# Second layer of a graph kernel: the one-hots of a row move from SBUF to a PSUM bank, but for the last sixteen rows

## The reference

```python
x = _layernorm(x + _L0_gnn_ref(x, src, dst, edge_weight, L0_gnn_W), axis=-1)
x = _layernorm(x + _L1_gnn_ref(x, edge_index, edge_attr_9, L1_gnn_w0, ..., L1_gnn_w4), axis=-1)
```

## Time and profile before

| | |
|---|---|
| median of 3 runs | 4325.02 us (4324.73 to 4326.77) |
| the profiled execution | 4325.59 us, of which the span from first to last instruction 4323.8 us |
| mean granted TensorE clock | 0.752 of full speed |
| busy over the span | PE 56%, DVE 49%, ACT 33%, POOL 68% |
| second layer, first gather to last | from 1529 us to 4299 us |

### The profile page before, as it was taken

One profiled execution on the slowest core, in us unless ns is written; L12 is line 12 of the kernel. 1 busy time (PEld: TensorE's weight loads), 2 busy tenths in 40 slices (PEclk: granted clock), 3 DMA queues, 4 the chain that ended last, 5 costly groups with the idle time before them and its releaser, 6 DMA issues.

```text
span 4323.8 us, 55250 instructions
## 1 busy us (share of the span) xinstructions
PE 2407.8 (56%) x15332; PEld 2127.3 (49%) x15334; DVE 2119.4 (49%) x4356; ACT 1419.8 (33%) x2142; POOL 2955.5 (68%) x2887
## 2 busy tenths in 40 slices
PE   2200399999999934545444444454544454445555
PEld 1000399999999823434343434343434343434444
DVE  8999788888888732222222222222222222223333
ACT  5444466666666521111111111111111111112222
POOL 5100277777777567777777777777777777777775
PEclk6555699999999867767777767776777776767767
DMA  1000233333333322212122112111211221212222
GB/s 56 7 0 19 83 95 95 95 101 96 95 95 100 110 64 54 55 49 53 49 54 54 49 54 54 49 54 48 54 54 48 54 54 48 54 49 66 78 74 59
DMA packets 116447, 268.24 MB, mean 62 GB/s; under 512 B 50449, under 2 KB 50593, under 8 KB 115233
## 3 DMA queue, kind: packets, MB, share of 16 engines
q0 software_dynamic: 92080, 191.02, 16.6%
q1 hardware_dynamic: 19698, 68.09, 4.5%
q10 hardware_dynamic: 4608, 8.39, 0.5%
HBM read 252.30 MB, written 8.72 MB: 60 GB/s over the span
## 4 chain that ended last, share of the span: by engine, by line
POOL 48%; issue 15%; PE 1%; POOLq 0%; DMA 0%; DVE 0%; ACT 0%; DVEq 0%
POOL feat L1562 48%; PE quad L1727 1%; POOLq L1558 0%; DMA feat<-x,ids 0%; PE mixed L1739 0%; POOLq L1559 0%; ACT z_last L1666 0%; DVE group L1871 0%; DVE dst_col L1956 0%; POOLq L1552 0%; DVE z_last L1967 0%; DVE stats L1970 0%; POOLq L1556 0%; POOLq L1510 0%; DVE mv L1973 0%
## 5 line engine op out<-in xcount | busy, mean ns | idle before, releaser
L1562 POOL DMA_INDIRECT feat<-x,ids x2048 | 2146.5, 1048 | 636.4 <-issue 635.8
L1727 PE MATMUL quad<-attr_hot,feat 128*128 128x144 f32 x4096 | 926.3, 409 | 1407.0 <-DMA feat<-x,ids 854.2
L1727 PEld LDWEIGHTS quad<-attr_hot,feat 128*128 128x128 f32 x4096 | 862.7, 295 | 1479.4 <-issue 1476.9
L1871 DVE TENSOR_TENSOR group<-group,quad 128x504 f32 (+1 forms) x512 | 348.0, 680 | 1907.3 <-PE quad L1727 1869.3
L1137 POOL DMA_INDIRECT l_feat<-in_x,id_of x768 | 727.3, 947 | 601.2 <-ACT w_of L830 366.7
L1579 ACT ACTIVATE quad<-quad 128x1008 uint32<-128x1008 uint32 x258 | 256.6, 995 | 2030.3 <-DVE group L1871 2030.3
L1739 PE MATMUL mixed<-group,mix 128*128 128x384 f32 x1152 | 411.2, 514 | 17.9 <-DVE group L1871 17.9
L1039 DVE TENSOR_SCALAR keys<-swap,src_of,w_of 128x184 f32<-128x184 f32 x1024 | 326.9, 389 | 92.6 <-PE l_pre L1230 92.6
L1039 DVE TENSOR_SCALAR w_row<-swap,src_of,w_of 128x184 f32<-128x184 f32 x1024 | 327.3, 390 | 51.6 <-PE l_pre L1230 49.6
L1847 DVE TENSOR_TENSOR attr_hot<-hot,attr_e 128x2304 f32<-128x2304 f32 x128 | 327.5, 2559 | 4.4
L1739 PEld LDWEIGHTS mixed<-group,mix 128*128 128x128 f32 x1152 | 234.1, 208 | 169.4 <-issue 46.1
(11 more groups left out here) (249 smaller groups left out, 2390.7 us busy)
## 6 DMA issues: line engine op xcount, KB each, us to landing
place<-table SPq DMA_DIRECT2D x64, 640.0 KB
feat<-x,ids POOLq DMA_INDIRECT x2048, 2.5
l_feat<-in_x,id_of POOLq DMA_INDIRECT x768
attr_in<-in_edge_attr SPq DMA_DIRECT2D x18, 576.0 KB, 3.9
norm_x<-in_x SPq DMA_DIRECT2D x16, 256.0 KB, 2.7
x<-norm_z ACTq DMA_DIRECT2D x16, 256.0 KB, 2.4
x_t<-x SPq DMA_DIRECT2D x15, 256.0 KB, 2.8
out<-z_t ACTq DMA_DIRECT2D x15, 256.0 KB, 2.3
```

The source lines that it names most:

```text
L1562: pool.indirect_dma_start(feat[z][:, t, :], None, x1, bass.IndirectOffsetOnAxis(ap=ids[j // (O // 2)][:, c:c + 1], axis=0),).then_inc(feat ...
L1727: last = nc.tensor.matmul(bank[:, :, bass.ds(places[t % H], WIN)], feat[z % S][:, t, :], attr_hot[z % 2][:, t, :, :], start=False, stop=(t ...
L1871: nc.vector.tensor_tensor(to, to, quad[:, q, 0:NA * QUAD_WIN].rearrange("p (m n) -> p m n", m=NA), ALU.add).then_inc(quad_added, 1)
```

## The change

The tile `hot` becomes `late_hot` and is used only where `next_hots` is called from the last sixteen rows, which is for rows 114 to 127. For rows 0 to 113 the one-hots are written to the first 256 columns of the PSUM bank `y`, and the 16 numbers that they are compared with are read from the next 16 columns, which one small copy per pass fills from the constant. `turn_nodes`, which writes to the same bank, gets a wait in its first call: all of `hots` up to row 113 must be done. Everything else is as it was; `attr_hot` itself stays in SBUF.

```diff
-        hot = sb("hot", [P, R, WIN], F32)
+        late_hot = sb("late_hot", [P, R, WIN], F32)
...
         y = ctx.enter_context(nc.psum_tensor("y", [P, BATCH * P], F32))
+        loop_hot = y[:, 0:R * WIN].rearrange("p (t n) -> p t n", t=R)
+        loop_iota = y[:, R * WIN:R * WIN + WIN]
...
             def turn_nodes(w, u, e):
 
+                if e == 0:
+                    pe.wait_ge(hot_made, u + 3)
                 pe.wait_ge(acc_added, u + 2 - e % 2)
...
-            def hots(u, r, j, z):
-
+            def hots(u, r, j, z, late=False):
+
+                hot = late_hot[:] if late else loop_hot
+                iota = g.cst[:, C_IOTA:C_IOTA + WIN] if late else loop_iota
                 cols = bass.ds(r * R, R)
                 s3, s4 = [P, R, WIN], [P, R, NA, WIN]
                 by_tile = attr_e[:, :, j * R:(j + 1) * R].rearrange("p m t -> p t m")
                 dve.wait_ge(hot_made, u + 1)
-                nc.vector.tensor_tensor(hot[:], g.cst[:, C_IOTA:C_IOTA + WIN].unsqueeze(1).to_broadcast(s3),
+                nc.vector.tensor_tensor(hot, iota.unsqueeze(1).to_broadcast(s3),
                                         g.dst_rel[:, cols].unsqueeze(2).to_broadcast(s3),
                                         ALU.is_equal).then_inc(hot_step, 1)
                 dve.wait_ge(hot_step, u + 1)
-                nc.vector.tensor_tensor(attr_hot[z][:], hot[:].unsqueeze(2).to_broadcast(s4),
+                nc.vector.tensor_tensor(attr_hot[z][:], hot.unsqueeze(2).to_broadcast(s4),
                                         by_tile.unsqueeze(3).to_broadcast(s4), ALU.mult).then_inc(hot_made, 1)
...
+                nc.vector.tensor_copy(loop_iota, g.cst[:, C_IOTA:C_IOTA + WIN]).then_inc(iota_made, 1)
+                dve.wait_ge(iota_made, w + 1)
                 dve.wait_ge(attr_out, w * (2 * OCTETS) + 2)
                 for r in range(2):
                     hots(w * RN + r, r, r, r)
...
                     if r + 2 < RN:
-                        next_hots(r // O, r % O)
+                        next_hots(r // O, r % O, late=True)
```

More of the change, by code:

```diff
@@ L1461, in layer1 @@
         move_step = sem("move_step")
+        iota_made = sem("iota_made")
         l1_step = sem("l1_step")
@@ L1908, in _, with next_hots @@
             with passes(dve) as w:
-                def next_hots(o, j):
+                def next_hots(o, j, late=False):
                     if (j + 2) % O == 0:
@@ L1912, in next_hots @@
                     r = o * O + (j + 2)
-                    hots(w * RN + r, r, (j + 2) % O, j % 2)
+                    hots(w * RN + r, r, (j + 2) % O, j % 2, late)
                 def row(o, j, first=False):
```

## The result

The changed kernel takes 4139.07 us (median of 4 runs, 4138.42 to 4139.79), the kernel before 4325.9 us (4 runs). The ratio is 0.9568, with a 95% interval of 0.9551 to 0.9585: 187 us, 4.3%, less. The profiled execution has a span of 4138.0 us.

What follows compares the result with a forecast made beforehand. GpSimd's gathers were taken to bound the kernel, some held up by VectorE's multiply. 4325.6 - 186.9 + 0 = 4138.7 us, or 4138 us (-4.3%) against the median, range 4128 to 4153 us.

Steps and rivals of the forecast that it cites:

- What bounds the kernel: Stage from 1529 to 4300 us: it lasts as long as GpSimd's 2048 gathers and their gaps.
- The multiply of rows 0 to 113, -186.9 us: VectorE's multiply with one PSUM input holds no gather: gain 186.9 us, bounds 0 and 186.9.
- Rows 114 to 127 unchanged, 23.1 us: Last rows keep SBUF one-hots and 23.1 us of gather stretching over 14 multiplies; no change, range -6 to +10.
- PSUM costs VectorE nothing: VectorE's 114 compares and 114 multiplies: 2 ns more each from PSUM, hidden behind GpSimd.
- the second rival: Multiply still holds the gather and takes longer; a skill page's 65 ns from PSUM would make it +7 us; 3 in 100.
- my far bound: VectorE's compare and multiply both take twice as long, 3.0 us more a row, still hidden.
- Copy, wait in `turn_nodes`, TensorE: Copy falls into VectorE's 1.25 us idle time, row 112's wait finds the multiply done, TensorE keeps up: 0.
- One sign of being wrong: Profile after: GpSimd's line showing waits for TensorE would mean the prediction is wrong.
- The tail: From the last gather on, 24.8 us: same work, 3 us either way by TensorE's clock level.
- Still holds: Rival: the new multiply still holds up the gather, no change, 4325 us; 5 in 100.
- still holds and takes longer: Rival: multiply still holds the gather and lengthens, so slower, 4617 us at the far bound; 3 in 100.
- part is given back: Rival: an unseen bound, such as TensorE late or slower gather rhythm, leaves 4155 to 4316 us; 3 in 100.

Runs made afterwards that it cites:

- Run 1: Changed kernel, but the compare reads its sixteen numbers from SBUF, so only the multiply is changed: 4138.06 us, ratio 0.957 to the kernel before.
- run 2: Changed kernel, but the one-hots stay in SBUF and only the compare's sixteen numbers come from PSUM: 4322.92 us, ratio 0.9998 to the kernel before.
- Run 8: Changed kernel with the one-hots of rows 114 to 127 in the same PSUM bank too: 4116.62 us, ratio 0.9519 to the kernel before.
- Run 4: Changed kernel with each multiply done twice, same inputs and result: 4159.3 us, ratio 0.9618 to the kernel before.
- run 3: Changed kernel with the two inputs of the multiply exchanged: 4141.13 us, ratio 0.9576 to the kernel before.
- run 5: Kernel before the change with each multiply done twice, all in SBUF: 4505.94 us, ratio 1.0422 to the kernel before.
- run 9: Changed kernel plus a copy of 2048 SBUF numbers to SBUF behind each multiply: 4207.65 us, ratio 0.9729 to the kernel before.
- run 10: Changed kernel plus a maximum over 2048 SBUF numbers behind each multiply: 4138.06 us, ratio 0.9569 to the kernel before.
- runs 6, 7: Kernel before the change with the multiply cut into 2, and into 8, all in SBUF: 4180.87 us, ratio 0.9666, and 4164.28 us, ratio 0.9627.

## Why the prediction was right

- **What bounds the kernel.** GpSimd's gathers did, and still do: the 187 us are gone from their line (2146.5 - 1960.3 = 186.2 us) and nowhere else, by the table.
- **The multiply of rows 0 to 113, -186.9 us.** The term was right in mechanism and size. Run 1 gives it to the multiply alone, run 2 shows that nothing comes without it. The about 1 us given to the compare can't be seen in totals (run 1 is 1.0 us below the changed kernel, inside the spread), though run 1 shows that a compare with two SBUF inputs does hold a gather.
- **Rows 114 to 127 unchanged, 23.1 us.** The page gives 27.0 us beyond the usual, of which 3.2 are the four gathers before 1539 us; 23.8 us are left, well inside -6 to +10. As forecast, there are 14 long gathers there and four at the start. Run 8 took the 14 away and gained 22.5.
- **PSUM costs VectorE nothing.** 2557 ns against 2558, and 425 against 419. The further 65 ns an instruction of the second rival did not appear. Run 4 shows the cover: a whole further multiply a row, 2.6 us, is hidden, close to my far bound of 3.0 us.
- **Copy, wait in `turn_nodes`, TensorE.** All at 0 for the total. The copy did not fall into VectorE's idle time, as the prediction had it; it came behind it, and the first compare started 0.41 us after the copy did:

```profile
1539.48 0.18 DVE L1941 COPY y<-cst 128x16 f32<-128x16 f32 x1 [1.13 <-issue]
1539.89 0.43 DVE L1850 TENSOR_TENSOR y<-y,dst_col 128x256 f32<-128x256 f32 x1 [0.23 <-DVE y L1941]
```

That is the bare case, under 0.5 us, which the prediction also had, and GpSimd did not wait for it. One sign of being wrong that the prediction named, waits for TensorE on GpSimd's line, did come up, 12 in place of 2; but each lasted 0.3 us, as every gap does, so nothing was lost to TensorE, and the sign was badly put. A `mix` takes up to 9.00 us in the trace of before, not 8.86; that makes 25.7 us of a pair of rows in place of 25.6 and changes nothing.
- **The tail.** 4138.0 - 4112.5 = 25.5 us from the start of the last gather, against 4323.8 - 4298.3 = 25.5. TensorE's granted clock did the same in both: 0.53 and 0.54 of full speed over 6 us around the last half row, near the lower of its two levels (1.2 GHz), where it took 4.18 us, and 1.00 over 8 us around the last `mix`, the upper level (2.4 GHz), where that took 6.04 us.
- **The rivals.** "Still holds" fell by the timeline and by run 3; "still holds and takes longer" needs both and neither is there; "part is given back" fell by the table. The rule of the Trainium skill that spoke against the change, SBUF — State Buffer, section "Who interferes with whom", infers that two SBUF inputs don't hinder the making of descriptors. Runs 2 and 5 contradict it for gathers: 1.6 us a row. The same section's other rule, a second SBUF input holds up a GpSimd instruction that reads SBUF, fits runs 1 to 8. What it says of fast copies, a lock until the copy's end, run 9 shows too.

What stays open: which of its reads or writes a gather is stopped at. The two distances, 0.81 and 0.11 us, say that there are two points, an early one that a second SBUF input or a fast copy closes, and a late one that of the instructions seen here only a fast copy closes. That the early one is the read of the node numbers and the late one the writing of descriptors is argued, not shown.

## What to carry to other kernels

When an engine issues indirect DMAs back to back and bounds the kernel, look at the spread of their durations, not their mean, and set the long ones beside what VectorE does at that moment: an end at a fixed distance behind the end of another engine's instruction points to something that the two share. VectorE need not do less for that: here the remedy was an instruction of another kind, with one input in PSUM. Where no bank is free, shorter instructions help: cutting the multiply in 2 took back two thirds of the loss with no change of layout. Work of VectorE of the harmless kind (at most one SBUF input, and no fast copy) is free up to its slack (2.6 us more a row in run 4, 2.3 in run 10).

## What the hardware showed that I had not expected

- A gather gets its turn between two VectorE instructions that each would hold it, with 0.03 us between them (run 5) or with none that the profile shows (runs 6, 7 and the last rows of 9). So the kernel with a train of eight short ones loses 57.3 us where the one with a single long one loses 213.2.
- A copy from SBUF to SBUF at 0.6 ns a number holds a gather that started up to some 0.4 us before the copy itself, until 0.11 to 0.13 us after the copy's end; a maximum over the same numbers, at 1.1 ns each, holds none.
- The compare takes some 7 ns more when its result goes to PSUM, and reading from the same bank adds nothing: it takes 425 ns with its sixteen numbers in that bank, 426 with them in SBUF (run 1), and 418 when only these numbers are in PSUM and the result is in SBUF (run 2).

```profile
L1850 DVE TENSOR_TENSOR y<-cst,dst_col 128x256 f32<-128x256 f32 x104 | 44.3, 426 | 0.0
```
```profile
L1850 DVE TENSOR_TENSOR late_hot<-y,dst_col 128x256 f32<-128x256 f32 x105 | 43.9, 418 | 0.0
```
